# Gated cross-attention with a routed expert layer: first context tiles loaded from ScalarE's queue

## The chip, the cores and the metric

One core of one Trainium2 chip. The metric is the device time of one execution in microseconds (us), as the median of several runs. TensorE (PE) does matmuls and transposes, VectorE (DVE), ScalarE (ACT) and GpSimd (POOL) the elementwise work. Loads and stores are issued by SyncE (SP), ScalarE or GpSimd and carried out by 16 DMA engines that all queues share. Engines run side by side and wait for one another through semaphores.

## The reference

`fake_quant` is clip(round(x / s + z), 0, 255), then (q - z) * s. `x` is (2, 512, 1024), the context (2, 1024, 1024), both float32; there are 8 experts with a 1024 x 1024 weight matrix each, and every token uses the best two.

```python
def _L0_xattn_ref(x1, x2, x1_scale, x1_zp, x2_scale, x2_zp):
    q1 = fake_quant(x1, x1_scale, x1_zp)
    q2 = fake_quant(x2, x2_scale, x2_zp)
    return jnp.matmul(q1, q2)

def _L0_ffn_ref(x, W_gate, b_gate, W_e, b_e):
    logits = x @ W_gate + b_gate
    _, top_idx = jax.lax.top_k(logits, 2)
    y_all = jax.nn.relu(jnp.einsum('bsd,edh->bseh', x, W_e) + b_e)
    y = jnp.take_along_axis(y_all, top_idx[..., None], axis=2)
    return y.mean(axis=2)

x = x + jnp.tanh(g_xattn[0]) * _L0_xattn_ref(_layernorm(x), ctx_4096, ...)
x = x + jnp.tanh(g_ffn[0]) * _L0_ffn_ref(_layernorm(x), ...)
```

## The kernel before, in words

The program has two parts. The first computes the quantised attention product and the routing, tile by tile: x is 8 tiles of 128 tokens by 1024 (NT = 8, 4 for each batch entry, TPB = 4), the context 16 tiles of 128 by 1024 (KT = 8 for each batch entry), each tile 512 KB. The second is a loop over slots of 128 gathered tokens, each with the weights of one expert (L953 has its matmuls). Every engine has its order of work written out by hand.

All of x stays in the chip. Context tiles go through `stage`, which has six places for them (CB = 6): `load_ctx(k)` (L227 to L230) writes place k % 6, and from k = 6 on it waits until tile k - 6 has been quantised (`s_uc`). `load_x(i)` is L232.

SP's list is: two quantiser scalars of x1 (L236), then x0, ctx0, x1, ctx1, x2, ctx2, x3, ctx3 (L237 to L239), ctx4 to ctx7 (L240), x4 to x7, the gate weights `wg` (L244), ctx8 to ctx15 (L245), and, once the last context tile is quantised (L253), the weights of expert 0 (L255) and two biases.

ScalarE's queue holds five small loads ahead of all its computing: x2's scale and zero point, the two gates (L418) and the gate bias `bg` (L419). Each is broadcast to 128 partitions: 4 bytes for each partition, 32 for `bg`. All four quantiser scalars count on one semaphore, `s_par`; the two gates and `bg` count on `s_gpar`.

VectorE begins with a wait for all four quantiser scalars (L563), computes their inverses (L564 to L567, `s_inv`), and then the layernorm statistics of x0, x1 and x2 (L584 to L586, each waiting for its tile), the scales of tiles 0 and 1 (`scales`, L599 to L606, which waits for ScalarE's square root), the quantised tiles 0 and 1 (L615, L619), and only then x3.

ScalarE's order after the issues is the following. Quantisation of context tile k is L426, the square root L432, the copy of the transposed tile L437. An activation function that isn't in the current table costs a table load first.

```python
act.wait_ge(s_inv, 1)
quantise_ctx(0)
act.wait_ge(s_gpar, 16 * 3)
act.activation(drv[:, TX:TF + 1], par[:, 4:6], ACT.Tanh).then_inc(s_tanh, 1)
quantise_ctx(1)
std(0, 0, 2, 1)
quantise_ctx(2)
quantise_ctx(3)
keep_q1T(0)
```

GpSimd centres each quantised context tile (L311). PE transposes the four quantised x tiles of the first batch entry (L822), then forms the column sums of its context (L833), and then the attention products (L847). The functions that the change touches, and what calls them:

Of the kernel before, what the change touches and what calls it, by code (L numbers as in the profile page):

```python
# [5 lines left out]
def flamingo_gated_moe(nc, x, ctx_kv, g_xattn, g_ffn, x1_scale, x1_zp, x2_scale, x2_zp,  # L6
# [16 lines left out]
    KT = D // P  # L23
    NT = B * S // P
    TPB = S // P
# [16 lines left out]
    ctx_t = ctx_kv.rearrange("b (k p) d -> (b k) p d", p=P)  # L42
# [5 lines left out]
    with ctx:  # L48
# [3 lines left out]
        def sem(name):  # L52
            return ctx.enter_context(nc.semaphore(name))
# [6 lines left out]
        def at(name, shape, dt, off):  # L60
            return nc.alloc_sbuf_tensor_at(name, shape, dt, offset=base + off)
# [5 lines left out]
        stage = at("stage", [P, KT, D], f32, STG)  # L67
# [12 lines left out]
        CB = 6  # L80
# [71 lines left out]
        s_ctx = [sem(f"ctx_landed{i}") for i in range(CB)]  # L152
# [64 lines left out]
        def entry(eng, field, slot, hi, lo=0):  # L217
            return eng.value_load(tab[0:1, bass.ds(slot + field, 1)], min_val=lo, max_val=hi)

        def settle(eng):  # L220

            eng.sem_inc(s_settled, 1)


        @block.sync
        def _(sp):
            def load_ctx(k):  # L227
                if k >= CB:
                    sp.wait_ge(s_uc, k - CB + 1)
                sp.dma_start(stage[:, k % CB, :], ctx_t[k]).then_inc(s_ctx[k % CB], 16)  # L230

            def load_x(i):  # L232
                sp.dma_start(xt[:, i, :], x_t[i]).then_inc(s_x[i], 16)

            for c, src in enumerate((x1_scale, x1_zp)):
                sp.dma_start(par[:, c:c + 1], src.partition_broadcast(P)).then_inc(s_par, 16)  # L236
            for i in range(TPB):  # L237
                load_x(i)
                load_ctx(i)  # L239
            for k in range(TPB, KT):  # L240
                load_ctx(k)
            for i in range(TPB, NT):
                load_x(i)
            sp.dma_start(wg[:, :, :], W_gate.rearrange("(k p) e -> p k e", p=P)).then_inc(s_wg, 16)  # L244
            for k in range(KT, 2 * KT):  # L245
                load_ctx(k)

            def store_x_new(i):
                sp.wait_ge(s_oa, i + 1)
                sp.dma_start(out_t[i], xt[:, i, :]).then_inc(s_oi, 16)  # L250


            sp.wait_ge(s_uc, B * KT)  # L253
            for c in range(NLO):
                sp.dma_start(stage[:, CK * c:CK * (c + 1), :], w_t[:, 0, CK * c:CK * (c + 1), :]).then_inc(s_w[c], 16)  # L255
            for e in range(2):
                sp.dma_start(bias[:, e * D:(e + 1) * D], b_e[e].partition_broadcast(P)).then_inc(s_bias[e], 16)
            for i in range(TPB):
                store_x_new(i)
            sp.wait_ge(s_xc, NT)  # L260
            sp.dma_start(stage[:, CK * NLO:, :], w_t[:, 0, CK * NLO:, :]).then_inc(s_w[NLO], 16)
            for i in range(TPB, NT):
                store_x_new(i)
            with sp.Fori(1, E) as n:
                for c in range(NCH):
                    sp.wait_ge(s_hi, n * NCH - NCH + c + 1)
                    settle(sp)
                    sp.wait_ge(s_lo, n * NCH - NCH + c + 1)
                    sp.dma_start(stage[:, CK * c:CK * (c + 1), :],
                                 w_t[:, bass.ds(n, 1), CK * c:CK * (c + 1), :].rearrange("p e k h -> p (e k) h")  # L270
                                 ).then_inc(s_w[c], 16)
                with sp.If(n > 1):
                    sp.wait_ge(s_post, entry(sp, BAS - 1, n, MAX_SLOTS, lo=1))
                    settle(sp)
                    for q in range(2):
                        with sp.If((n & 1) == q):
                            sp.dma_start(bias[:, q * D:(q + 1) * D],
                                         b_e[bass.ds(n, 1), :].rearrange("a d -> (a d)").partition_broadcast(P)
                                         ).then_inc(s_bias[q], 16)
                    sp.nop()  # L280
                sp.nop()
# [132 lines left out]

        @block.scalar
        def _(act):
            for c, src in enumerate((x2_scale, x2_zp, g_xattn, g_ffn)):
                act.dma_start(par[:, c + 2:c + 3], src.partition_broadcast(P)).then_inc(s_par if c < 2 else s_gpar, 16)  # L418
            act.dma_start(bg[:, :], b_gate.partition_broadcast(P)).then_inc(s_gpar, 16)  # L419
# [566 lines left out]
```

## Time and profile before

| what | us |
|---|---|
| median of 3 runs | 419.95 |
| lowest and highest | 419.49, 422.17 |
| the profiled execution | 422.89 |
| its span, from the first to the last instruction | 421.2 |
| PE busy | 327.9 (78%) |
| DVE busy | 228.7 (54%) |
| POOL busy | 147.3 (35%) |
| ACT busy | 137.1 (33%) |

Times in the trace count from the span's start. L12 is line 12 of the kernel. A name with q (SPq, ACTq) is an engine's queue at the issue of a DMA. "idle before, releaser" is the time for which an engine stood still before an instruction and what ended that. "Us to landing" of a DMA is counted from its issue to its completion. Of the DMA queues, q1 is SP's and q10 ScalarE's.

### The profile page before, as it was taken

The page shows a single profiled execution, that of the slowest core. Times are in us where ns is not written, and L with a number is a line of the kernel's source. Part 1 is how long each engine was busy: PE and PEld are TensorE (multiplying, and loading weights), DVE is VectorE, ACT ScalarE, POOL GpSimd, SP SyncE. Part 2 cuts the span into 40 slices and gives each one's busy share as a digit, 9 for nine tenths or more (in the row PEclk, how much of TensorE's full clock was granted, in tenths as well). Part 3 has the DMA queues.
Part 4 walks back from the last instruction along what each step waited for, and adds up shares of the span by engine and source line. Part 5 has one row for each costly group of instructions (what it writes and reads, how often), then busy time and mean ns, then how long its engine had stood idle before and what let it go on. Part 6 is the DMA issues. An engine that isn't in the chain of part 4 may idle for free.

```text
span 421.2 us, 6706 instructions
## 1 busy us (share of the span) xinstructions
PE 327.9 (78%) x1680; PEld 258.5 (61%) x1687; DVE 228.7 (54%) x294; ACT 137.1 (33%) x115; POOL 147.3 (35%) x147
## 2 busy tenths in 40 slices
PE   0029488696853439999997997999999999999950
PEld 0014256263643438888886785888888877888840
DVE  1796875268896918435966753076222921862210
ACT  1565466615532007004551700071002600700000
POOL 2422654492588021122214412223133322533320
PEclk9999978898955558999999699899999999999995
DMA  4993121489259245935999596459444994444442
GB/s 150 406 389 154 51 100 52 169 358 321 100 205 340 105 137 191 321 78 123 310 362 396 174 337 165 100 125 391 138 100 96 267 374 102 111 95 100 98 95 50
DMA packets 23869, 81.46 MB, mean 193 GB/s; under 512 B 4017, under 2 KB 4017, under 8 KB 23857
## 3 DMA queue, kind: packets, MB, share of 16 engines
q1 hardware_dynamic: 15792, 54.56, 34.7%
q0 software_dynamic: 6192, 22.55, 23.5%
q10 hardware_dynamic: 1872, 4.20, 2.5%
q8 instruction: 6, 0.10, 0.1%
q14 instruction: 7, 0.05, 0.0%
HBM read 62.43 MB, written 18.87 MB: 193 GB/s over the span
## 4 chain that ended last, share of the span: by engine, by line
PE 52%; DVE 17%; DMA 12%; issue 7%; ACT 5%; POOL 1%; DVEq 1%; SPq 1%; POOLq 1%; ACTq 0%
PE ps L953 40%; DMA out_dram<-res,sidx 4%; PE ps_y L930 4%; PE ps L847 3%; DMA stage<-in_L_ffn_W_e_dram 3%; DVE lnv L600 3%; DMA xt<-in_x_dram 2%; DMA y_rows<-y_scratch,gidx 2%; PE ps L833 2%; DVE st L584 2%; PE ps_s L881 1%; PE ps_q L822 1%; DVE xt L625 1%; ACT y L451 1%; DVE lnv L601 1%
## 5 line engine op out<-in xcount | busy, mean ns | idle before, releaser
L953 PE MATMUL ps<-w_hi,yT_hi 128*128 x320 | 102.8, 403 | 3.1 <-issue 2.5
L953 PE MATMUL ps<-w_lo,yT_hi 128*128 x320 | 100.8, 397 | 0.0
L953 PE MATMUL ps<-w_hi,yT_lo 128*128 x320 | 100.4, 395 | 0.0
L805 DVE TENSOR_TENSOR res<-ps,bias 128x1024 f32<-128x1024 f32 x20 | 24.5, 1224 | 111.0 <-PE ps L953 110.1
L528 ACT ACTIVATE yT_hi<-ps_y 128x1024 fp32r<-128x1024 f32 x21 | 21.6, 1027 | 189.1 <-PE ps_y L930 189.1
L953 PEld LDWEIGHTS ps<-w_hi,yT_hi 128*128 128x128 f32 x320 | 60.1, 193 | 15.5 <-issue 4.1
L953 PEld LDWEIGHTS ps<-w_lo,yT_hi 128*128 128x128 f32 x320 | 61.4, 192 | 13.2
L953 PEld LDWEIGHTS ps<-w_hi,yT_lo 128*128 128x128 f32 x320 | 61.3, 192 | 13.2
L779 DVE TENSOR_TENSOR w_lo<-stage,w_hi 128x2048 f32 x28 | 62.6, 2287 | 8.5 <-ACT w_hi L544 8.2
L375 POOL COPY gidx<-idx 128x1 uint32 x23 | 4.6, 201 | 145.7 <-issue 101.5
L544 ACT ACTIVATE w_hi<-stage 128x2048 f32 x28 | 51.7, 1907 | 6.0 <-DMA stage<-in_L_ffn_W_e_dram 6.0
L401 POOL DMA_INDIRECT out_dram<-res,sidx x20 | 36.7, 1835 | 35.6 <-DVE res L807 22.7
L378 POOL DMA_INDIRECT y_rows<-y_scratch,gidx x23 | 28.6, 1242 | 18.7 <-POOL gidx L375 18.7
L930 PE MATMUL ps_y<-ident_f,y_rows 128*128 128x128 f32 x168 | 23.8, 288 | 13.5 <-DMA y_rows<-y_scratch,gidx 10.8
L847 PE MATMUL ps<-q,q1T 128*128 128x512 bf16 x123 | 32.3, 418 | 0.6 <-issue 0.4
L773 DVE TENSOR_TENSOR yT_lo<-ps_y,yT_hi 128x1024 fp32r<-128x1024 f32 x21 | 25.7, 1222 | 12.7 <-ACT yT_hi L528 12.7
L930 PEld LDWEIGHTS ps_y<-ident_f,y_rows 128*128 128x128 f32 x168 | 20.6, 148 | 17.3 <-DMA y_rows<-y_scratch,gidx 7.9
L822 PE MATMUL ps_q<-ident_b,q 128*128 128x128 bf16 x64 | 6.5, 263 | 31.4 <-DVE q L619 26.5
L311 POOL TENSOR_SCALAR q<-u8c 128x1024 bf16<-128x1024 uint8 x16 | 16.9, 1059 | 35.4 <-ACT u8c L426 35.3
L822 PEld LDWEIGHTS ps_q<-ident_b,q 128*128 128x128 bf16 x64 | 5.0, 119 | 32.0 <-issue 22.6
L847 PEld LDWEIGHTS ps<-q,q1T 128*128 128x128 bf16 x128 | 13.8, 109 | 17.4 <-issue 6.3
L584 DVE BATCH_NORM_STATS2 st<-xt 128x6 f32<-128x512 f32 x32 | 20.6, 685 | 6.1 <-DMA xt<-in_x_dram 5.7
(120 smaller groups left out, 313.3 us busy)
## 6 DMA issues: line engine op xcount, KB each, us to landing
stage<-in_L_ffn_W_e_dram SPq DMA_DIRECT2D x32, 1024.0 KB, 8.5
stage<-in_ctx_dram SPq DMA_DIRECT2D x16, 512.0 KB, 8.8
xt<-in_x_dram SPq DMA_DIRECT2D x8, 512.0 KB, 10.3
y_scratch<-y ACTq DMA_DIRECT2D x8, 512.0 KB, 2.6
bias<-in_L_ffn_b_e_dram SPq DMA_DIRECT2D x8, 512.0 KB, 6.0
out_dram<-xt SPq DMA_DIRECT2D x8, 512.0 KB, 3.1
y_rows<-y_scratch,gidx POOLq DMA_INDIRECT x23
out_dram<-res,sidx POOLq DMA_INDIRECT x20, 6.3
```

The lines of the kernel that those rows point to most:

```text
L311: pool.tensor_scalar(q2[:, k, :], u8c[:, k % 2, :], 1.0, -QMID, ALU.mult, ALU.add).then_inc(s_q2, 1)
L378: pool.indirect_dma_start(out=y_rows[q][:, :], out_offset=None, in_=y_dram[:, :], in_offset=bass.IndirectOffsetOnAxis(ap=gidx[:, q:q + 1], ...
L401: pool.indirect_dma_start(out=out_rows[:, :], out_offset=bass.IndirectOffsetOnAxis(ap=sidx[:, q:q + 1], axis=0), in_=res[q][:, :], in_offs ...
L528: act.activation(yT_hi[q][:, :, :], ps_y[:, :, :], ACT.Copy).then_inc(s_eh, 1)
L544: act.activation(w_hi[:, bass.ds(dst + c * CW, CW)], stage[:, CK * c:CK * (c + 1), :].rearrange("p k h -> p (k h)"), ACT.Copy).then_inc(s_ ...
L584: last = dve.bn_stats(st[:, which, h, :], xt[:, i, h * 512:(h + 1) * 512])
L773: dve.tensor_tensor(yT_lo[q][:, :, :], ps_y[:, :, :], yT_hi[q][:, :, :].bitcast(f32), ALU.subtract).then_inc(s_el, 1)
L779: dve.tensor_tensor(w_lo[:, dst], stage[:, CK * c:CK * (c + 1), :].rearrange("p k h -> p (k h)"), w_hi[:, dst].bitcast(f32), ALU.subtract) ...
L805: dve.tensor_tensor(res[q][:, :], ps[q][:, :], bias[:, bass.ds(woff >> 3, D)], ALU.add).then_inc(s_free, 1)
L847: last = pe.matmul(ps[u % 2][:, h * 512:(h + 1) * 512], q1T[:, i, k, :], q2[:, b * KT + k, h * 512:(h + 1) * 512], start=(k == 0), stop=(k ...
L930: last = pe.transpose(ps_y[:, k, :], y_rows[q][:, k * P:(k + 1) * P], ident_f[:, :])
L953: last = pe.matmul(ps[q][:, h * 512:(h + 1) * 512], lhs[q][:, k, :], w[:, bass.ds(woff + k * D + h * 512, 512)], start=(k == 0 and lhs is ...
```

## The change

ScalarE issues the loads of the six first context tiles, ahead of its five small loads. SP issues x0 to x3 one behind the other, and its context loads start with tile 6. Nothing else is different.

```diff
--- before.py
+++ after.py
@@ -236,8 +236,7 @@
                 sp.dma_start(par[:, c:c + 1], src.partition_broadcast(P)).then_inc(s_par, 16)
             for i in range(TPB):
                 load_x(i)
-                load_ctx(i)
-            for k in range(TPB, KT):
+            for k in range(CB, KT):
                 load_ctx(k)
             for i in range(TPB, NT):
                 load_x(i)
@@ -414,6 +413,8 @@
 
         @block.scalar
         def _(act):
+            for k in range(CB):
+                act.dma_start(stage[:, k, :], ctx_t[k]).then_inc(s_ctx[k], 16)
             for c, src in enumerate((x2_scale, x2_zp, g_xattn, g_ffn)):
                 act.dma_start(par[:, c + 2:c + 3], src.partition_broadcast(P)).then_inc(s_par if c < 2 else s_gpar, 16)
             act.dma_start(bg[:, :], b_gate.partition_broadcast(P)).then_inc(s_gpar, 16)
```

## Rows read from the trace of the kernel before

**Rows 1.** The page: the chain that ended last, share of the span by engine.
```profile
PE 52%; DVE 17%; DMA 12%; issue 7%; ACT 5%; POOL 1%; DVEq 1%; SPq 1%; POOLq 1%; ACTq 0%
```

**Rows 2.** The chain in order of time, 0 to 40 us: start, us, what.
```profile
4.73 9.91 DMA xt<-in_x_dram
...
16.30 0.18 DVE lnv L599
...
33.01 5.84 PE ps L833 x16
```

**Rows 3.** Timeline of ScalarE: start us, us, engine, line, what [idle before, releaser].
```profile
8.88 1.28 ACT L426 ACT_TABLE_LOAD   x1 [8.76 <-DMA stage<-in_ctx_dram]
10.18 1.24 ACT L426 ACTIVATE u8c<-stage,par,drv 128x1024 uint8<-128x1024 f32 x1
11.72 0.20 ACT L481 ACTIVATE drv<-par 128x2 f32<-128x2 f32 x1 [0.30 <-DMA bg<-in_L_ffn_b_gate_dram]
13.36 1.24 ACT L426 ACTIVATE u8c<-stage,par,drv 128x1024 uint8<-128x1024 f32 x1 [1.43 <-DMA stage<-in_ctx_dram]
...
15.91 0.30 ACT L432 ACTIVATE lnv<-mv,eps 128x2 f32<-128x2 f32 x1
```

**Rows 4.** Timeline of VectorE, its first instructions.
```profile
5.66 0.16 DVE L564 RECIPROCAL drv<-par 128x1 f32<-128x1 f32 x1 [5.54 <-DMA par<-in_L_xattn_x_zp_dram]
...
7.34 1.29 DVE L584 BATCH_NORM_STATS2 st<-xt 128x6 f32<-128x512 f32 x2 [1.35 <-DMA xt<-in_x_dram]
8.66 0.21 DVE L586 BATCH_NORM_AGGREGATE mv<-st 128x2 f32<-128x12 f32 x1
```

**Rows 5.** ScalarE's small loads: issues (start, us), then count, KB, us to landing.
```profile
0.85 0.41 ACTq L418 DMA_DIRECT2D par<-in_L_xattn_x_scale_dram  x1
1.29 0.46 ACTq L418 DMA_DIRECT2D par<-in_L_xattn_x_zp_dram  x1
...
2.74 0.45 ACTq L419 DMA_DIRECT2D bg<-in_L_ffn_b_gate_dram  x1
...
par<-in_L_xattn_x_zp_dram ACTq DMA_DIRECT2D x1, 0.5 KB, 4.3
...
bg<-in_L_ffn_b_gate_dram ACTq DMA_DIRECT2D x1, 4.0 KB, 9.0
```

**Rows 6.** SP's issues of x7 and wg, their landing, and ctx14's, issued alone at 33.01.
```profile
16.41 0.43 SPq L233 DMA_DIRECT2D xt<-in_x_dram  x1
16.89 0.43 SPq L244 DMA_DIRECT2D wg<-in_L_ffn_W_gate_dram  x1
...
xt<-in_x_dram SPq DMA_DIRECT2D x1, 512.0 KB, 12.7
wg<-in_L_ffn_W_gate_dram SPq DMA_DIRECT2D x1, 32.0 KB, 12.5
...
stage<-in_ctx_dram SPq DMA_DIRECT2D x1, 512.0 KB, 3.9
```

**Rows 7.** Queues: packets, MB; at 2 to 2.5 us, 5 to 11, 27 to 27.5.
```profile
q10 hardware_dynamic: 63, 0.00, 7.1%
...
q1 hardware_dynamic: 465, 1.67, 75.2%
q10 hardware_dynamic: 443, 0.01, 3.7%
...
DMA packets 653, 0.12 MB, mean 236 GB/s; under 512 B 629, under 2 KB 629, under 8 KB 653
```

**Rows 8.** Stretches: PE, PEld, DVE, ACT, POOL busy, clock, DMA share, GB/s.
```profile
5.00:11.00 6.00, 0.00 (x0) 0.00 (x0) 1.83 (x7) 2.10 (x2) 0.00 (x0) 1.00 0.79 279
...
13.00:26.00 13.00, 2.02 (x16) 1.55 (x16) 10.45 (x28) 9.84 (x11) 4.44 (x5) 1.00 1.03 414
```

**Rows 9.** VectorE's statistics of x4; SP's wait ahead of the expert weights.
```profile
31.06 1.28 DVE L584 BATCH_NORM_STATS2 st<-xt 128x6 f32<-128x512 f32 x2
...
SPq L255 <- ACT u8c L426: 23.5, 1, 23.5
```

## The prediction

> **What bounds the kernel now.** I read the chain of work that ended last first, then the timelines of ScalarE and VectorE over the first 20 us, then the DMA view cut into short stretches. The chain as a whole [rows 1] is matmuls of the expert loop for the most part, but it has a serial head, and the change lies in that head. Followed in order of time [rows 2], the chain starts with the loads: it waits for x until 14.6 us (x tile 2), then runs through VectorE's statistics and, at 16.30, the first `lnv` reciprocal (L599), which needs ScalarE's square root, and reaches the column sums on PE at 33.01. From there it is engine work all the way to the expert loop. So what the change does is read at one point: when does L599 start, now 16.30?
>
> Two things come together there. VectorE needs x0, x1, x2 and 1.29 + 0.21 us of statistics for each [rows 4]. ScalarE reaches its square root [rows 3] through a fixed row of steps: table load 1.28, quantise ctx0 1.24, wait for the gate scalars and tanh 0.20 (at 11.72, released by `bg`), quantise ctx1 1.24 (at 13.36, when ctx1 had landed), a second table load that fills the 1.3 us up to 15.91, square root 0.30. Both ends are at 16.2. And in front of all of it stands the wait for the four quantiser scalars: VectorE does nothing before 5.66 [rows 4], when x2's zero point has landed, and ScalarE's first quantisation needs VectorE's inverse.
>
> **What the change removes.** Four of the six context loads leave SP's list ahead of x3 and two after it. SP then issues x0 to x3 with nothing in between. SP's issues of a tile cost 0.43 us each [rows 6], and they are not what x waits for: x2 was issued at 4.73 and its wait lasts 9.91 us [rows 2], so it is the transfers in front of it. With two queues full, the engines take packets from both in turn: between 5 and 11 us SP's queue had 465 packets and ScalarE's 443 [rows 7], though the one carried 4 KB packets and the other tiny ones. With context tiles in the other queue, x_i is again paired with one context tile each, as it was in SP's list. So x2 gains at most what the tiny packets took (279 GB/s instead of 414 over 6 us [rows 8], 0.8 MB, or 2 us); it would land at about 12.5 instead of 14.6. That is worth something only if nothing else is later.
>
> The Trainium skill, page "DMA: Bandwidth & Descriptors", section "Issuing engines are not separate DMA queues", says that issuing from several engines saves the issue time alone, since all transfers run on the same 16 engines. By that rule the move itself would give back six issues of 0.43 us at most and no bandwidth; no row here shows two bulk queues of loads at once, and the sum below does not use the rule.
>
> **What the change adds, and where it hurts.** The six context loads go ahead of all of ScalarE's small loads, in the same queue. These are x2's scale and zero point (both needed by VectorE before its first instruction), then both gates and `bg` (needed before tanh, which is ahead of ctx1's quantisation and the square root). Before, x2's zero point landed 4.3 us after its issue at 1.29 and `bg` 9.0 after its own at 2.74 [rows 5]: at 5.6 and 11.7. After, 3.15 MB stand in front of them. That a queue keeps its order is seen on SP: the 32 KB of `wg`, issued at 16.89, took 12.5 us to land, at 29.4, right behind x7 (issued 16.41, 12.7 us, landed 29.1) [rows 6].
>
> When is ctx5 through? ScalarE's queue moves its first packets at 2.0 us, 1.15 us after the first issue at 0.85 [rows 5, 7]; at the pace of the first small load (63 packets in half a microsecond) ctx0's packets would be through at 3.2, and I let it be 4.0, since they are large. The nine other tiles in both queues (ctx1 to ctx5, x0 to x3) are 4.72 MB, at the 414 GB/s of the full stretch [rows 8] 11.4 us: 15.4. A lone tile lands 3.9 us after its issue [rows 6], of which 1.15 is the start and 1.27 the data, so 1.5 us is the tail: ctx5 lands at 16.9. The small loads wait in the queue by then for ten microseconds. How fast do they follow? The nearest row for small packets behind a backlog is `wg`: 629 packets of under 512 B moved within half a microsecond, and it landed 0.3 us after the tile ahead of it [rows 6, 7]. A scalar load has 144 packets. So I take 0.3 us for the two scalars together, and another 0.4 for the three gate loads: P = 17.2 for the quantiser scalars, G = 17.6 for `bg`.
>
> From P the steps of [rows 3] run with nothing to hide them: 0.45 (VectorE's four small operations and the hand-over), table load 1.3, ctx0 1.24, tanh with its gaps 0.26 (G has passed), ctx1 1.25 (landed long ago), table load 1.3, square root 0.3, hand-over 0.1: P + 6.2 = 23.4. VectorE is ready at P + 0.4 + 3 x 1.55 = P + 5.1, so ScalarE is the later one. L599 starts at 23.4 instead of 16.30: 7.1 us late. Bounds of the rate: the packet pairs of 5 to 11 us cost 6 us x 16 / 454 = 0.21 us each, a lone 4 KB packet at 414 GB/s with its share of the completions 0.14; if the missing 0.07 is the turning between two queues and not the tiny packet, each of the some 72 packets per engine of eight paired tiles costs 0.03 more, 2.2 us in all, and the delay is 9.3. I take 7.5, near the low end.
>
> **What becomes of the delay.** No later load takes it up or adds to it. ctx6 now waits for ctx0's quantisation (P + 3.0 = 20.2) and, with a lone tile's 3.9, lands at 24; it is quantised after 24 + 7. x4 to x7 stand behind ctx7, which waits for ctx1's quantisation at P + 4.6 = 21.8; even with the longest landing of 12.7 us x4 is there at 34.5, and VectorE reads it at 31.06 + 7 = 38 [rows 9]. The expert weights are issued only when the last context tile is quantised (SP waits 23.5 us for that [rows 9]), so they shift with the rest. Chain steps after L599 wait for one another and for no clock on the wall, so I carry the 7.5 us in full. What is not in it: where POOL's work falls beside VectorE's tiny operations: I allow a microsecond either way.
>
> The profiled execution took 422.89 us for a span of 421.2; with 7.5 it would be 430.4. It lies 2.9 above the median of the three runs, so on the median of 419.95 the forecast is 427.5.
>
> **Rivals.**
> (a) The small loads stay slow behind the backlog too. For it: on ScalarE's queue `bg` landed three loads and 6.1 us behind x2's zero point, so 2 us for each, though they had been issued within 1.5 us [rows 5]. Against it: that was beside big packets in the other queue, packet for packet, and in the changed kernel SP's queue is empty then. At 1.9 us apiece P = 20.7 and G = 16.9 + 9.5 = 26.4; now G decides, the square root is done at G + 3.1 = 29.5, and the delay is 13.2: 433.1. The Trainium skill, same page, section "Anatomy of one DMA", gives a DMA about 2.0 us of fixed cost and puts most of it down to completion, which in a full queue would overlap; taken as paid one after the other it would give an estimate of 433.4, taken as overlapping it is the main forecast.
> (b) Not slower: the small loads don't wait for the context tiles, because ScalarE's queue doesn't hold its order against transfers that spread over all engines. Then `bg` is there at about 11.7 as before, ctx1 has landed already, so tanh, ctx1, table load and square root end at 11.72 + 3.1 = 14.8; x2 is there at 12.5 and VectorE is ready by 14.1. L599 starts 1.4 us earlier: 418.5. The rows of `wg` speak against it; it decides if x2's zero point lands before about 10 us.
> (c) The context queue gets more than its half, so that the six tiles are through by about 12 and x lands last. P = 12.5, square root at 18.7, x2 by 15: delay 2.4, 422.4. The even packet counts of [rows 7] speak against it.
>
> **Chances.** Main forecast 0.60, (a) 0.22, (b) 0.04, (c) 0.06, and 0.08 for a later loss on top of the main case, such as the expert loop's loads meeting otherwise. A measurement of this kernel tells about 1% (4.2 us) from no change. Main forecast, (a) and the last give slower; (b) and (c) lie within 1%; faster by over 1% would need more than 4.2 us before 16.2 with `bg` at 11.7 in front of 3.1 us of ScalarE's steps, which can't be from this head. The range holds the main case with its bounds of rate and reaches just over (a): 424.5 to 433.5.
>
> **What would show it.** In the changed kernel's timeline VectorE's first reciprocal should start near 17, released by the load of x2's zero point; L599 near 23.5; the small loads should land within a microsecond of one another, and ctx5 just ahead of them. VectorE's waits for x should be gone, since x0 to x3 are there before the scalars. The column sums should start near 40.5, and the expert loop take as long as before. Wrong for (a): small loads 2 us apart and tanh long after the reciprocal. Wrong for (b): the reciprocal still near 6.

## The result and the profile after

The changed kernel takes 431.75 us (median of 4 runs, 430.89 to 432.36) against 420.03 us for the kernel before (4 runs, 419.49 to 422.17): a ratio of 1.0268, with a 95% interval of 1.0228 to 1.0307. It was measured twice more, beside other kernels, six runs against 17 of the kernel before each time: 1.0204 (1.0157 to 1.0252) and 1.0217 (1.0170 to 1.0265). The change makes the kernel 2 to 2.7% slower, 8 to 12 us. The profiled execution took 432.36 us, its span is 430.6.

The place to look is the head. The chain of work that ended last, 0 to 60 us, in order of time (start, us, what), of the changed kernel:

```profile
2.75 1.14 ACTq L417
...
3.92 0.71 ACTq L417
...
4.65 0.49 ACTq L419
...
5.17 13.32 DMA par<-in_L_xattn_x_zp_dram
...
41.00 5.17 PE ps L834 x16
```

Where [rows 2] had 9.91 us of waiting for x, it has now 13.32 us of waiting for 0.5 KB, x2's zero point. It was issued at 5.17, behind ctx5 at 3.92, and landed at 18.5. The timelines of VectorE and ScalarE, the lines that answer to [rows 4] and [rows 3]:

```profile
18.52 0.16 DVE L565 RECIPROCAL drv<-par 128x1 f32<-128x1 f32 x1 [18.40 <-DMA par<-in_L_xattn_x_zp_dram]
...
18.89 1.29 DVE L585 BATCH_NORM_STATS2 st<-xt 128x6 f32<-128x512 f32 x2
...
20.45 1.29 DVE L585 BATCH_NORM_STATS2 st<-xt 128x6 f32<-128x512 f32 x2
...
22.02 1.29 DVE L585 BATCH_NORM_STATS2 st<-xt 128x6 f32<-128x512 f32 x2
...
23.58 0.17 DVE L600 RECIPROCAL lnv<-lnv 128x2 f32<-128x2 f32 x1
```

```profile
7.41 1.28 ACT L427 ACT_TABLE_LOAD   x1 [7.28 <-issue]
18.89 1.24 ACT L427 ACTIVATE u8c<-stage,par,drv 128x1024 uint8<-128x1024 f32 x1 [10.20 <-DVE drv L568]
20.04 0.19 ACT L482 ACTIVATE drv<-par 128x2 f32<-128x2 f32 x1
20.13 1.22 ACT L427 ACTIVATE u8c<-stage,par,drv 128x1024 uint8<-128x1024 f32 x1
21.37 1.28 ACT L433 ACT_TABLE_LOAD   x1
22.66 0.30 ACT L433 ACTIVATE lnv<-mv,eps 128x2 f32<-128x2 f32 x1
```

VectorE stands still for 18.4 us, then works through x0, x1 and x2 with no gap between them: no x tile is waited for any more. ScalarE takes its first table load at 7.41, in the time in which it has nothing to do, and then waits 10.2 us for VectorE's inverse. The reciprocal that was at 16.30 (L599, here L600) is at 23.58, 7.28 us later.

The DMA issues of ScalarE's small loads (count, KB, us to landing), which answer to [rows 5], and the issue of ctx5 alone:

```profile
par<-in_L_xattn_x_scale_dram ACTq DMA_DIRECT2D x1, 0.5 KB, 13.4
par<-in_L_xattn_x_zp_dram ACTq DMA_DIRECT2D x1, 0.5 KB, 13.3
par<-in_g_xattn_dram ACTq DMA_DIRECT2D x1, 0.5 KB, 12.3
par<-in_g_ffn_dram ACTq DMA_DIRECT2D x1, 0.5 KB, 12.3
bg<-in_L_ffn_b_gate_dram ACTq DMA_DIRECT2D x1, 4.0 KB, 12.9
...
stage<-in_ctx_dram ACTq DMA_DIRECT2D x1, 512.0 KB, 14.2
```

With their issues at 4.65, 5.17, 5.79, 6.32 and 6.83 they landed at 18.1, 18.5, 18.1, 18.6 and 19.7; ctx5 at 3.92 + 14.2 = 18.1. The queues between 8 and 16 us (packets, MB, share of the 16 engines) and then in the half microseconds from 16.5 and from 18:

```profile
q1 hardware_dynamic: 454, 1.66, 51.5%
q10 hardware_dynamic: 451, 1.65, 51.1%
...
q10 hardware_dynamic: 279, 0.07, 63.7%
...
q10 hardware_dynamic: 60, 0.00, 5.5%
```

Two queues of big tiles share evenly, packet for packet, and together move the 414 GB/s that one alone moved [rows 8]. Behind them the first small packets go at 279 in half a microsecond, the last ones at 60.

In these two profiles nothing takes the delay up later on. The first gather of the expert loop, in the chain before and then in GpSimd's timeline after:

```profile
147.00 4.40 DMA y_rows<-y_scratch,gidx
```

```profile
154.75 1.18 POOL L377 DMA_INDIRECT y_rows<-y_scratch,gidx  x1 [0.93 <-POOL gidx L374]
```

### The profile page after: what moved, and what is told of

Read it like the earlier page. It is cut to its first block, busy times and chain, and to the rows that moved or that the text cites. A ratio compares the mean times of both kernels' runs of the same rounds, so it can differ in the third digit from the quotient of the medians.

```text
span 430.6 us, 6706 instructions
## 1 busy us (share of the span) xinstructions
PE 328.9 (76%) x1680; PEld 258.4 (60%) x1687; DVE 225.3 (52%) x294; ACT 136.7 (32%) x115; POOL 147.5 (34%) x147
## 4 chain that ended last, share of the span: by engine, by line
PE 51%; DVE 17%; DMA 13%; issue 7%; ACT 6%; ACTq 2%; POOL 1%; DVEq 1%; POOLq 1%; SPq 0%
PE ps L954 39%; DMA out_dram<-res,sidx 4%; PE ps_y L931 4%; PE ps L848 3%; DMA par<-in_L_xattn_x_zp_dram 3%; DMA stage<-in_L_ffn_W_e_dram 3%; DMA y_rows<-y_scratch,gidx 2%; DVE lnv L601 2%; DVE st L585 2%; ACT y L452 1%; PE ps L834 1%; ACT u8c L427 1%; DVE lnv L602 1%; PE ps_s L882 1%; PE ps_q L823 1%
## 5 line engine op out<-in xcount | busy, mean ns | idle before, releaser
L954 PEld LDWEIGHTS ps<-w_hi,yT_hi 128*128 128x128 f32 x320 | 59.7, 192 | 15.4 <-issue 4.2
L931 PE MATMUL ps_y<-ident_f,y_rows 128*128 128x128 f32 x168 | 24.7, 295 | 15.6 <-DMA y_rows<-y_scratch,gidx 13.0
L848 PE MATMUL ps<-q,q1T 128*128 128x512 bf16 x123 | 33.6, 431 | 0.6 <-issue 0.4
L931 PEld LDWEIGHTS ps_y<-ident_f,y_rows 128*128 128x128 f32 x168 | 21.3, 152 | 19.7 <-DMA y_rows<-y_scratch,gidx 7.9
L848 PEld LDWEIGHTS ps<-q,q1T 128*128 128x128 bf16 x128 | 14.2, 112 | 18.5 <-issue 8.1
L336 POOL TENSOR_TENSOR w_lo<-stage,w_hi 128x2048 fp32r<-128x2048 f32 x4 | 18.5, 4648 | 12.9 <-ACT w_hi L466 12.9
```

What stands on the lines that cost most here:

```text
L336: pool.tensor_tensor(w_lo[:, c * CW:(c + 1) * CW], stage[:, CK * c:CK * (c + 1), :].rearrange("p k h -> p (k h)"), w_hi[:, c * CW:(c + 1) ...
L848: last = pe.matmul(ps[u % 2][:, h * 512:(h + 1) * 512], q1T[:, i, k, :], q2[:, b * KT + k, h * 512:(h + 1) * 512], start=(k == 0), stop=(k ...
L931: last = pe.transpose(ps_y[:, k, :], y_rows[q][:, k * P:(k + 1) * P], ident_f[:, :])
L954: last = pe.matmul(ps[q][:, h * 512:(h + 1) * 512], lhs[q][:, k, :], w[:, bass.ds(woff + k * D + h * 512, 512)], start=(k == 0 and lhs is ...
```

## The experiments

Theory W: the small loads wait in ScalarE's queue behind the context tiles; VectorE's start hangs on the quantiser scalars and ScalarE's square root on the gates, and whatever that delays is carried to the end. Rival T: the transfers themselves are slower or land in a worse order with two queues. The ratios are against runs of the kernel before on the same chip; its median there was 422.96 beside e1, e2, e4 and e5, 421.4 beside e3, e6, e7 and the second measurement of the changed kernel, and 421.94 beside e8, e9 and the third.

**1. The small loads first (e1).** ScalarE's issues in the changed kernel, reordered:

```diff
-            for k in range(CB): ... ctx_t[k]
             for c, src in enumerate((x2_scale, x2_zp, g_xattn, g_ffn)): ...
             act.dma_start(bg[:, :], ...)
+            for k in range(CB): ... ctx_t[k]
```

> The changed kernel with ScalarE's five small loads issued ahead of its six context loads; SP's list as in the change. Theory W (the small loads wait behind the context tiles, nothing else matters): VectorE's first reciprocal back near 5.7 us, bg back near 11.7; but the context tiles now stand behind the slow small loads, so ctx0 lands near 13 and ctx1 near 15, L599 (line 600 or so here) starts at 17.5 to 18.5, and the time is 421 to 422.5. Rival T (the loss comes from two queues of big tiles, by which x0 landed at 10.3 instead of 7.3): the time stays above 428.

Measured: 426.74 us, ratio 1.0102 (1.0050 to 1.0153). That is 3.8 us over the median of before, where the changed kernel lies 8.2 to 11.7 over it: by the medians more than half of the loss is gone, though less than I expected (421 to 422.5 on a median of 420, 1 to 2.5 over). VectorE's reciprocal is back at 5.86, and ScalarE's timeline shows the new bound:

```profile
13.97 1.28 ACT L427 ACT_TABLE_LOAD   x1 [13.84 <-DMA stage<-in_ctx_dram]
```

ctx0 landed at 13.9, behind the five small loads; the square root follows at 19.05 and the reciprocal after it at 19.44, a microsecond later than I had put it, 3.1 us later than before. Rival T, as the main cause, is out: it needed 428 or more. On ScalarE's queue either the small loads wait or the tiles do.

**2. Which of the small loads (e2, e3).** The one kernel has only the gates and `bg` behind the tiles (this diff), the other the reverse, only x2's scale and zero point behind them:

```diff
+            for c, src in ((0, x2_scale), (1, x2_zp)): ...
             for k in range(CB): ... ctx_t[k]
-            for c, src in enumerate((x2_scale, x2_zp, g_xattn, g_ffn)): ...
+            for c, src in ((2, g_xattn), (3, g_ffn)): ...
             act.dma_start(bg[:, :], ...)
```

> The changed kernel with x2's scale and zero point ahead of the six context loads and only the two gates and bg behind them. Theory W with both waits (the gate loads, by tanh ahead of ctx1's quantisation, hold the square root as much as the quantiser scalars hold VectorE): reciprocal near 6, bg near 19.5, L599 at bg + 3.1 = 22.7, time only some 1 us under the changed kernel, 430 to 431.5. Rival (the quantiser scalars are the whole loss): L599 near 17, time 421 to 422. Rival T: as the changed kernel, but with tanh not released by bg.

> The changed kernel with the two gates and bg ahead of the six context loads and only x2's scale and zero point behind them. Theory W with both waits: bg lands near 10, then the context tiles, the zero point near 19.5 (the tiles start later than in the changed kernel, the gate loads being slow beside x); VectorE's first reciprocal 19.5 to 21, L599 5.1 us after it, 24.5 to 26, so 8 to 10 us slower than before. If only the gates mattered: L599 below 18.

Measured: gates behind 430.30 us, ratio 1.0163 (1.0108 to 1.0218); scalars behind 433.52 us, ratio 1.0288 (1.0241 to 1.0336). Both losses are there alone, and they don't add up. ScalarE's timeline with the gates behind, and VectorE's with the scalars behind:

```profile
20.99 0.20 ACT L484 ACTIVATE drv<-par 128x2 f32<-128x2 f32 x1 [9.46 <-DMA bg<-in_L_ffn_b_gate_dram]
```

```profile
21.64 0.16 DVE L567 RECIPROCAL drv<-par 128x1 f32<-128x1 f32 x1 [21.53 <-DMA par<-in_L_xattn_x_zp_dram]
...
26.70 0.17 DVE L602 RECIPROCAL lnv<-lnv 128x2 f32<-128x2 f32 x1
```

With the gates behind, VectorE starts at 6.27 and has the statistics of x2 done by 15.4, and waits all the same until 24.04 for the square root: tanh stands ahead of it on ScalarE and needs `bg`, which landed at 20.9 (I had 19.5).

```profile
24.04 0.17 DVE L602 RECIPROCAL lnv<-lnv 128x2 f32<-128x2 f32 x1 [8.65 <-ACT lnv L435]
```

So moving the quantiser scalars alone to the front of the list would have saved nothing at this place: the reciprocal after the square root is at 24.04, in the changed kernel at 23.58. With the scalars behind it is at 26.70, 5.1 us after VectorE's first reciprocal as the theory has it, but both reciprocals came 0.6 to 0.7 us later than I allowed, and the time is 12 us over before where I had 8 to 10.

**3. Nothing but a late start (e4).** The kernel before, all loads as they were, with extra work on VectorE that nothing reads:

```diff
             dve.wait_ge(s_par, 16 * 4)
+            link(dve.memset(bias[:, :], 0.0))
+            for _ in range(5):
+                link(dve.tensor_tensor(pad[:, :], bias[:, :], bias[:, :], ALU.add))
```

> The kernel before with every load as it was, and on VectorE, after its wait for the scalars, 12.9 us of extra work that nothing reads (one memset and five adds of 2048 elements), so that its first reciprocal starts at about 18.5 as in the changed kernel. If the late start is all (theory W), L599 is at 23.6 and the time that of the changed kernel, 430.5 to 432.5. If the change also loses something by its transfers, or later for a reason of its own, this one ends at 427 to 429.

Measured: 431.02 us, ratio 1.0183 (1.0129 to 1.0237). The added work came out a little long:

```profile
19.51 0.16 DVE L568 RECIPROCAL drv<-par 128x1 f32<-128x1 f32 x1
...
24.57 0.17 DVE L603 RECIPROCAL lnv<-lnv 128x2 f32<-128x2 f32 x1
```

A reciprocal 8.27 us late (24.57 against 16.30) costs 8.1 us between the medians. That is one for one within the interval (5.5 to 10.0 us), which wouldn't show a microsecond or two on top. With a reciprocal 1.0 us later than the changed kernel's (23.58), it reaches a loss of the same size without any change of loads.

**4. SP's new order alone (e5).** The kernel before with x0 to x3 ahead of ctx0 to ctx7, all on SP:

```diff
             for i in range(TPB):
                 load_x(i)
-                load_ctx(i)
-            for k in range(TPB, KT):
+            for k in range(KT):
                 load_ctx(k)
```

> The kernel before with SP's list reordered and nothing moved to ScalarE: x0 to x3, then ctx0 to ctx7. Theory W: small loads as before (reciprocal 5.7, bg 11.7); x0 to x3 land at about 7.3, 8.8, 11 and 13, ctx0 only at 14.7, ctx1 at 16; ScalarE then needs 5.6 us from ctx0, so L599 near 20.3 and the time 424. If x were what the head waits for, this would be faster than before: 417 to 419.

Measured: 426.60 us, ratio 1.0101 (1.0047 to 1.0155). x2's statistics start at 11.11 instead of 14.73, but ctx0 lands at 13.8 instead of 8.8, and the reciprocal, behind ScalarE's square root, is at 19.38 (forecast 20.3), 3.1 us late. The order hastens x and delays the context at once, so what x alone would be worth it doesn't show; an earlier x gains nothing when ctx0, which ScalarE needs before its square root, comes later for it.

**5. Two tiles ahead instead of six (e6).**

```diff
-            for k in range(CB): ... ctx_t[k]      (ScalarE)
+            for k in range(2): ... ctx_t[k]       (ScalarE; ctx2 to ctx5 on SP)
```

> The changed kernel with two context tiles (ctx0, ctx1) on ScalarE's queue ahead of its small loads, ctx2 to ctx5 on SP behind x3. Dose of theory W: two tiles ahead instead of six; ctx1 lands near 7.9 as in the changed kernel, and the small loads then go packet for packet beside x, 2 us each: zero point near 11.5 to 12.5, bg near 17.5 to 19. Now bg decides: L599 at bg + 3.1 = 20.5 to 22, 4 to 6 us slower than before. If small loads behind a tile were always quick (0.1 us each), bg would be at 9, L599 at 15.5 to 16.5, and the time as before.

Measured: 426.17 us, ratio 1.0108 (1.0062 to 1.0155). The small loads, with their landings:

```profile
par<-in_L_xattn_x_scale_dram ACTq DMA_DIRECT2D x1, 0.5 KB, 7.6
par<-in_L_xattn_x_zp_dram ACTq DMA_DIRECT2D x1, 0.5 KB, 8.5
par<-in_g_xattn_dram ACTq DMA_DIRECT2D x1, 0.5 KB, 9.4
par<-in_g_ffn_dram ACTq DMA_DIRECT2D x1, 0.5 KB, 10.1
bg<-in_L_ffn_b_gate_dram ACTq DMA_DIRECT2D x1, 4.0 KB, 11.4
```

Issued at 1.78 to 4.55, they landed at 9.4, 10.8, 12.2, 14.0 and 16.0: 1.4 to 2 us apart, beside SP's tiles. The zero point came 0.8 us sooner than the early end of its forecast and `bg` 1.5 us sooner, and `bg` decides: tanh 15.99, reciprocal 19.04, 2.7 us late (forecast 4.2 to 5.7), with 4.8 us between the medians. The dose is there: two tiles ahead cost 1.1%, six 2 to 2.7%. The loss of 4.8 us is 2.0 more than the reciprocal's delay, for which the run gives no cause.

**6. The gates in SP's list, near its head and further back (e7, e9).** The kernel before with both gates and `bg` issued by SP, behind x0 and ctx0 in the first, behind ctx5 in the second:

```diff
                 load_x(i)
                 load_ctx(i)
+                if i == 0:
+                    for c, src in ((4, g_xattn), (5, g_ffn)): sp.dma_start(...)
+                    sp.dma_start(bg[:, :], ...)
```

> The kernel before with the gates and bg taken off ScalarE's queue and put into SP's list behind x0; nothing else moved. Theory W and its finding that small loads are slow only beside a full second queue: from 5.7 us on SP's queue is alone, the three loads cost it some 0.3 us, x2 lands near 12.5 instead of 14.6 and ctx1 near 11 instead of 13.4, L599 near 14.2 instead of 16.30, the time 2 us under before (0.5%). If the small loads are as slow in SP's queue (2 us each), x1 and all behind it land later by 6 us and L599 is at 19 or later.

> The kernel before with both gates and bg in SP's list behind ctx5, where they wait some ten microseconds for their turn (behind x0 in e7: some six). If small loads become quick when they have been in the queue for long, as behind six tiles in the changed kernel, the three cost SP's stream under 1.5 us in all and bg lands within 1.5 us of ctx5; if they take 1.1 to 2 us each wherever they stand, bg lands 3.5 us or more behind it. ctx5 near 19.5; x2 and ctx1 land 1.5 to 2 us earlier than before, since no small load runs beside them. L599 follows bg by 3.1 us, 23 to 26, so the time is 6 to 9 us over before.

Measured: near the head 421.78 us, ratio 1.0022 (0.9989 to 1.0055), no difference; behind ctx5 430.69 us in a single run, 8.8 over the median of before, with the reciprocal at 23.29, 7.0 late. The gain of 2 us that I expected from the first isn't there. VectorE's statistics of x1 in the two:

```profile
12.62 1.29 DVE L587 BATCH_NORM_STATS2 st<-xt 128x6 f32<-128x512 f32 x2 [3.77 <-DMA xt<-in_x_dram]
```

```profile
10.00 1.29 DVE L588 BATCH_NORM_STATS2 st<-xt 128x6 f32<-128x512 f32 x2 [0.98 <-DMA xt<-in_x_dram]
```

Behind x0 and ctx0 the three loads held up SP's stream from about 8 to 10.7 us, so that x1 came at 12.6; they landed at 8.6, 10.1 and 11.3. Behind ctx5, issued at 7.30 to 8.27, they landed at 19.0, 19.3 and 20.3. ctx5 landed at 18.9 (issued at 6.82, 12.1 us), so `bg` came 1.4 us behind it: the branch for loads that become quick when they have been in the queue for long. The packets of SP's queue in half a microsecond, at 8.5 in the first kernel and at 18 in the second:

```profile
q1 hardware_dynamic: 36, 0.00, 3.2%
```

```profile
q1 hardware_dynamic: 334, 0.08, 74.9%
```

So it is not a second queue alone that makes small loads slow, as I had it: with ScalarE's queue empty they went at 32 to 75 packets in half a microsecond between 8.5 and 10.5 us, too. Those behind ctx5 came at 279 (the changed kernel) and 334 (here) in one half microsecond. With the gates out of the way the statistics of x1 and x2 began at 10.0 and 12.56, 1.2 and 2.2 us sooner than before; only `bg` at 20.3 makes nothing of it.

**7. The head reordered (e8).** The experiments say that square root and reciprocal wait for things they don't use: ctx1 on ScalarE, x2 on VectorE. The kernel before, with its loads as they were:

```diff
-            quantise_ctx(1)
             std(0, 0, 2, 1)
+            quantise_ctx(1)
...
             x_stats(1)
-            x_stats(2)
             scales(0, 0, 2, 1)
             quantise_x(0)
             quantise_x(1)
+            x_stats(2)
             x_stats(3)
```

> The kernel before with its loads as they were and the head's work reordered: ScalarE takes the first square root before ctx1's quantisation, VectorE makes the scales and quantised tiles 0 and 1 from x0 and x1 before it takes the statistics of x2. If the head is bound as the experiments on the waits say (after bg at 11.7 ScalarE needs tanh, table load and square root, 1.9 us; after x1's statistics at 12.7 VectorE needs nothing of x2), L599 starts at 13.6 to 14 instead of 16.30, the column sums some 1.5 to 2.5 us earlier, and the time is 1.5 to 2.5 us under before (ratio 0.994 to 0.997). If x2 and x3 are needed as early as before in any case, L599 moves and the column sums don't, and the time is that of before.

Measured: 420.59 us (12 runs) against 421.94 (17 runs), ratio 0.9981 (0.9952 to 1.0011).

```profile
13.52 0.17 DVE L599 RECIPROCAL lnv<-lnv 128x2 f32<-128x2 f32 x1 [0.81 <-ACT lnv L432]
...
23.65 0.17 DVE L599 RECIPROCAL lnv<-lnv 128x2 f32<-128x2 f32 x1
```

The reciprocal is 2.8 us earlier; the second one, for tiles 2 and 3, is only 1.2 us earlier (24.81 before), as x2's and x3's statistics now stand behind tiles 0 and 1 on VectorE. The column sums start at 31.84, 1.2 us earlier too (forecast 1.5 to 2.5), and the first gather is at 143.97 in its profile. The medians agree in sign and size, but the interval holds 1: a gain of this size isn't shown.

**8. The changed kernel again (in e3's group and e10).** For the size of the loss, unchanged, in the last two groups:

> The changed kernel itself once more, beside the other kernels and on their chip. In its profile the head is 7.3 us late at L599 and 7.8 at the expert loop's first matmul; the medians of the first measurement lay 11.7 us apart. If the delay is carried one to one as in e1, e2, e4 and e5 (3.1, 7.7, 8.3 and 3.1 us late at L599 for about 3.5, 7.3, 8.0 and 3.5 us on the median of before), it is now 7.3 to 8.5 us slower than before. If the change loses some 3 us more by something of its own, it is 10.5 to 12.5 us slower again.

> The changed kernel a third time, for the size of the loss: the first measurement gave 11.7 us between the medians (four runs a side), the second 8.2 (six and seventeen). If the head's 7.3 to 7.8 us are carried one to one, with a microsecond or so on top from where the later waits fall, it is 7.5 to 9.5 us.

Measured: 429.63 us (ratio 1.0204) and 431.07 us (1.0217), 8.2 and 9.1 us over the medians of before, both within what was expected. Their first gathers are at 152.88 and 153.60; from there to the end of the span it takes 273.5 and 274.8 us, 275.9 in the first profile and 274.2 in the kernel before. Over all these kernels this rest lies between 272.0 and 278.1 us whatever was done to the head.

All kernels side by side, in us. The first two columns are against the one profile of before (16.30 and 147.00), the third is between the medians:

| kernel | reciprocal late | first gather late | time over before |
|---|---|---|---|
| e8 | -2.8 | -3.0 | -1.4 |
| e7 | 0.5 | -2.1 | 0.4 |
| e6 | 2.7 | 3.1 | 4.8 |
| e5 | 3.1 | 1.7 | 3.6 |
| e1 | 3.1 | 1.9 | 3.8 |
| e9 (one run) | 7.0 | 7.8 | 8.8 |
| changed kernel | 7.3 | 7.8 | 11.7 |
| again | 7.4 | 5.9 | 8.2 |
| third | 7.5 | 6.6 | 9.1 |
| e2 | 7.7 | 8.0 | 7.3 |
| e4 | 8.3 | 7.7 | 8.1 |
| e3 | 10.4 | 9.9 | 12.1 |

The time follows the reciprocal. But for the first measurement of the changed kernel, every kernel that is later at the reciprocal loses between 0.4 us less and 2.0 more than its delay there.

## Why the prediction was right, and where not

The direction, the mechanism and the place were right, and the median lies in the range, 4.25 us above the forecast of 427.5. That it does is in part the width of the range: the main case with its own bound of rate (9.3 us) ended at 429.3, and only the reach to rival (a) takes 431.75 in. The two later measurements, 8.2 and 9.1 us, lie within that bound. Step by step:

- **What comes together at L599.** Right. Experiment 2 (e2, e3) shows both ways into it, and experiment 4 (e5) that x sooner with ctx0 later makes it late.
- **ctx5 through.** Forecast 16.9, measured 18.1. The step that was too small is the start: I let ctx0 be through at 4.0 and have all data at full pace from there. ctx0 landed at 0.85 + 5.1 = 6.0, and x1's zero point went beside it, packet for packet, until 6.4, so x0 began late and landed at 10.3 instead of 7.3. The other half of that step, 414 GB/s for two queues of tiles, was right, and so the bound of 9.3 us for turning between queues was empty.
- **The small loads behind the backlog.** Forecast 0.3 us for the two scalars, measured 0.4 (18.1 to 18.5). `bg` took 1.6 after ctx5 instead of 0.7. It didn't decide here: tanh ran at 20.04, when ctx0's quantisation was done. Rival (a), whose time of 433.1 lies nearer to the first median than mine, has its mechanism refuted by this: it needed the scalars 3.8 us behind ctx5 and `bg` 9.5. Its second estimate, with 2.0 us for each load one after the other, comes to 433.7 by its own steps and not 433.4. The section of the Trainium skill's page "DMA: Bandwidth & Descriptors" that it names, "Anatomy of one DMA", gives the 2.0 us for DMAs that GpSimd issues; ScalarE's here, all five of them, landed within 1.6 us.
- **From P to L599.** Forecast P + 6.2 by ScalarE, measured P + 5.1 by VectorE. I had the first table load after the scalars; it needs nothing of them and ran at 7.41. ScalarE was done at 22.96, P + 4.5, and VectorE's three statistics were the later. That L599 came out so near (forecast 23.4, or 23.8 with the 0.4 added, measured 23.58) is luck: 1.3 us too few in P and 1.1 too many here cancel.
- **Carried in full.** In the first profile the column sums on PE are at 41.00 instead of 33.01, the first gather is 7.75 us late and the span 9.4 longer. In the two later profiles the gather is only 5.9 and 6.6 us late for 7.4 and 7.5 at L600, so the stretch up to it varies by a microsecond or two as well. Experiment 3 (e4) confirms one for one within its interval.
- **The total.** 7.5 forecast; 11.7, 8.2 and 9.1 measured. The term that was too small is what is added behind the head, which I put at nothing with a microsecond either way. A part of it is the sample: behind the first gather the profiles vary by up to 6 us, and only the first measurement is well over 2 us above its delay at L600. Whether a microsecond or two is real stays open: e3, e6 and the third measurement have 1.6 to 2.0 on top, e2 and e4 none, and the intervals overlap.

The rival on the other side, (b), and rival (c) are out: the queue kept the small loads behind the tiles, and the tiles shared evenly with x.

## What to carry to other kernels

A load's place in its queue is its due time. Before bulk is put at the head of a list, ask of every small load behind it which engine cannot begin without it, and how much else stands in order behind that engine's wait: half a kilobyte cost 8 us here. And where two inputs of a step come late together, hastening the one at the other's cost (x, in experiment 4, e5) buys nothing; look at what an engine waits for out of order rather than out of need. Here that moved the reciprocal 2.8 us (experiment 7, e8), though a gain in the kernel's time isn't shown.

## What was unexpected in the hardware

- Small broadcast loads (144 packets each with their completions) are not slow because of a second queue alone: in e7, alone on the engines and some six microseconds after their issue, they landed 1.2 to 1.5 us apart. Behind six tiles the changed kernel's first four landed within 0.6 us, in e2 all three within 0.6 us, and in e9 the first two within 0.3. The last one was slower in the changed kernel and in e9 (`bg` 1.1 and 1.0 us behind its neighbour), and in e3 the two scalars, though queued for 11 us, landed 1.3 us apart. That some packets are made ready ahead of their turn would fit most of this; no run here separates making them from moving them, and the rule stays open.
- Within one queue loads don't land strictly in the order of their issues. In e3 ctx5 was issued at 8.00 and landed at 21.3; x2's scale, issued behind it at 8.69, landed at 20.3, a microsecond ahead of it, and the zero point at 21.6. In the changed kernel the first gate landed at 18.1, before the zero point (18.5) that was issued ahead of it. The rows of e3:

```profile
8.00 0.66 ACTq L420 DMA_DIRECT2D stage<-in_ctx_dram  x1
...
stage<-in_ctx_dram ACTq DMA_DIRECT2D x1, 512.0 KB, 13.3
par<-in_L_xattn_x_scale_dram ACTq DMA_DIRECT2D x1, 0.5 KB, 11.6
par<-in_L_xattn_x_zp_dram ACTq DMA_DIRECT2D x1, 0.5 KB, 12.4
```

- Two queues with 4 KB packets lose nothing against one: 454 and 451 packets in 8 us, 414 GB/s together.
- A table load can run ahead of a wait of its activation: in the changed kernel it came at 7.41, when ctx0 had landed and ScalarE's issues were out, without VectorE's inverse, 11.5 us before the quantisation that it serves. The kernel of experiment 3 (e4) shows the same with the loads as before: table load at 8.87, when ctx0 had landed, quantisation at 19.88. In e3 it was at 12.61, 9.4 us ahead of its quantisation.
